# The state recurrence of a decoder layer: how the product with C is formed and summed

## The reference, cut to what matters

```python
proj = hidden_states @ W_in.T                      # 512 -> 2 x 1024
x, gate = (proj[..., :D_IN], proj[..., D_IN:])
...                                                # causal convolution of 4 taps
x = silu(xc)
ssm = x @ W_x.T                                    # 32 + 16 + 16 columns
ts, Bm, Cm = rms of each part
dt = softplus(ts @ W_dt.T + b_dt)
def step(state, inp):
    dt_t, B_t, C_t, u_t = inp
    dA = jnp.exp(dt_t[..., None] * A)
    state = state * dA + (dt_t * u_t)[..., None] * B_t[:, None, :]
    y = jnp.einsum('bdn,bn->bd', state, C_t)
    return (state, y)
y = ys + x * D
y = y * silu(gate)
return y @ W_out.T
```

## Time and profile before

| | |
|---|---|
| median of 3 runs | 1618.45 us (1616.8, 1620.61, 1618.45) |
| profiled execution, its own time | 1616.8 us, the lowest of the three runs |
| its span from first to last instruction | 1616.8 us, 14599 instructions |
| busy: PE, DVE, ACT, POOL | 1351.5, 1080.7, 595.1, 655.2 us |
| mean granted clock of PE | 0.936 |

### The profile page before, as it was taken

How to read it: one execution, slowest core, us unless ns; L and a number is a source line. 1 busy time by engine, 2 the same in 40 slices (tenths; PEclk the granted TensorE clock), 3 DMA queues, 4 the chain that set the end, 5 groups by cost and what they waited for, 6 DMA issues and landing times.

```text
span 1616.8 us, 14599 instructions
## 1 busy us (share of the span) xinstructions
PE 1351.5 (84%) x4824; PEld 805.4 (50%) x4824; DVE 1080.7 (67%) x1691; ACT 595.1 (37%) x1115; POOL 655.2 (41%) x469
## 2 busy tenths in 40 slices
PE   7956667678956757698889999979999999999996
PEld 5522222235512222244435555547887878877774
DVE  7399999938399999837865444346444446555566
ACT  4464343313454344202212322225444434444431
POOL 3276666513377676411117111135333333333321
PEclk9878998989869898999989999979999999999999
DMA  5320000012320000150011000013221112222110
GB/s 205 126 104 6 7 13 7 13 59 72 118 99 7 13 7 7 37 173 12 3 36 50 20 20 1 14 41 103 71 73 66 66 53 79 78 65 64 49 59 26
DMA packets 34169, 85.70 MB, mean 53 GB/s; under 512 B 3888, under 2 KB 4144, under 8 KB 31152
## 3 DMA queue, kind: packets, MB, share of 16 engines
q1 hardware_dynamic: 34096, 84.78, 15.7%
HBM read 82.54 MB, written 2.23 MB: 52 GB/s over the span
## 4 chain that ended last, share of the span: by engine, by line
PE 54%; DVE 15%; issue 5%; ACT 2%; POOL 1%; DMA 0%; POOLq 0%; DVEq 0%; ACTq 0%
PE psum L422 7%; PE psum L424 7%; PE psum L423 7%; DVE arena L1396 4%; PE psum L755 3%; DVE psum L1403 3%; PE psum L625 3%; PE psum L782 3%; PE psum L486 3%; PE psum L619 3%; PE psum L495 2%; PE psum L542 2%; PE psum L774 2%; DVE arena L1341 1%; PE psum L583 1%
## 5 line engine op out<-in xcount | busy, mean ns | idle before, releaser
L486 PE MATMUL psum<-arena,prm 128*128 128x512 f32 x512 | 289.2, 695 | 174.0 <-DVE arena L1396 173.4
L1145 POOL TENSOR_TENSOR arena<-arena 128x1024 f32<-128x1024 f32 x128 | 310.3, 2426 | 122.4 <-DVE psum L1403 121.1
L1403 DVE TENSOR_TENSOR_SCAN psum<-psum,arena 128x1024 f32<-128x1024 f32 x128 | 292.4, 2286 | 8.7 <-ACT psum L807 8.7
L1113 POOL TENSOR_TENSOR w_split<-arena,w_split 128x512 fp32r<-128x512 f32 x128 | 168.1, 1332 | 311.9 <-ACT w_split L807 311.8
L486 PEld LDWEIGHTS psum<-arena,prm 128*128 128x128 f32 x512 | 97.0, 210 | 366.1 <-DVE arena L1396 293.8
L807 ACT ACTIVATE arena<-psum 128x512 f32<-128x512 f32 (+2 forms) x180 | 101.4, 575 | 275.2 <-PE psum L511 62.5
L807 ACT ACTIVATE arena<-arena 128x512 f32<-128x512 f32 x112 | 69.2, 628 | 258.1 <-DVE arena L1609 224.0
L807 ACT ACTIVATE psum<-arena,amat 128x508 f32<-128x508 f32 x256 | 163.5, 670 | 0.0
L1396 DVE TENSOR_TENSOR arena<-psum,arena 128x1024 f32<-128x1024 f32 x128 | 154.7, 1209 | 0.5 <-PE psum L486 0.5
L807 ACT ACTIVATE arena<-psum,prm 128x512 f32<-128x512 f32 (+1 forms) x130 | 89.0, 696 | 127.4 <-PE psum L619 54.4
L1093 POOL TENSOR_TENSOR lnrs<-lnve,halfneg 128x1 f32<-128x1 f32 x48 | 29.9, 623 | 248.7 <-DVE lnve L1313 248.7
(11 more groups left out here) (218 smaller groups left out, 2382.5 us busy)
## 6 DMA issues: line engine op xcount, KB each, us to landing
arena<-bc_scratch SPq DMA_DIRECT2D x16, 1024.0 KB, 7.6
arena<-wq SPq DMA_DIRECT2D x64, 256.0 KB, 2.9
arena<-wo SPq DMA_DIRECT2D x64, 256.0 KB, 2.9
arena<-win SPq DMA_DIRECT2D x32, 256.0 KB, 2.7
arena<-wout SPq DMA_DIRECT2D x16, 256.0 KB, 2.6
arena<-xT SPq DMA_DIRECT2D x8, 256.0 KB, 5.4
x_tok<-xtok SPq DMA_DIRECT2D x1, 2048.0 KB, 7.8
arena<-ctxtok SPq DMA_DIRECT2D x1, 2048.0 KB, 8.8
```

The costliest lines, as they stand in the source:

```text
L486: last = mm(bank[6 + m % 2][:, :], ident, prod[:, i % 2, n, :], start=False, stop=(q == GS - 1 and n == NG - 1))
L1113: gp.tensor_tensor(out_, whole, hi.bitcast(F32), ALU.subtract).then_inc(done, 1)
L1145: gp.tensor_tensor(bu[:, i % 2, :, :], dtu[:, m % 2, :].unsqueeze(1).to_broadcast([P, NG, HT]), Brep[:, q * NG:(q + 1) * NG, :], ALU.mult) ...
L1403: v.tensor_tensor_scan(d, d, bu[:, i % 2, :, :].rearrange("p n t -> p (n t)"), 0.0, ALU.mult, ALU.add).then_inc(S.scan_done, 1)
```

## The change

The product with C no longer happens with channels on partitions. Each scanned state row is transposed by PE, so that time lies on partitions and C is one value per partition, and is scaled while it is copied out of PSUM. Then PE transposes it back and accumulates in PSUM in the same instruction.

A unit k is now one state row n of a pair of channel blocks (e = 0 and 1). There are 64 units in a pass, MP = 4 pairs of blocks by 16 rows.

- `Crep` and its four DMAs are gone; only B goes through DRAM.
- The scan (two of 512 columns per unit) reads `dA` in PSUM (three buffers of one bank) and writes `hst` in SBUF (four buffers). The zeros at the starts of the sequences are written once per pass instead of in each step, since the scan no longer overwrites them.
- `turn_state` on PE: eight transposes of 128 x 128 per unit, from `hst` to `hT`, three buffers of one bank, each with two of the four sequences. `weigh` scales them by `ssmn` into `hTs`: four operations of 128 x 256 per unit, on ACT, but in every fourth unit the second two are on DVE. `sum_state`: eight transposes back, accumulating in banks 6 and 7.
- The order on PE is turn (k, 0), sum (k-1), turn (k, 1), save where k % 16 is 1. The skip product comes after row 4 instead of first.
- `bu` has four buffers of 1024 columns and lies over the split weights, so POOL waits for the end of the input projection; `dtu` has four buffers; the gates of the two blocks of a pair come together.

The diff, cut to its core:

```diff
-dA = psum[:, 0:3 * NG * HT].rearrange("p (s n t) -> p s n t", s=3, n=NG)
+dA = psum[:, 0:3 * HT].rearrange("p (s t) -> p s t", s=3)
+hT = psum[:, 3 * HT:6 * HT].rearrange("p (s b e d) -> p s b e d", s=3, b=2, e=2)
 skip = sb("skip", [P, 2, P])
-zeros = sb("zeros", [P, NG * HB])
-bu = part(80, 2 * NG * HT).rearrange("p (s n t) -> p s n t", s=2, n=NG)
-prod = part(88, 2 * NG * HT).rearrange("p (s n t) -> p s n t", s=2, n=NG)
+zeros = sb("zeros", [P, 3 * HB])
+bu = part(40, 4 * NG * HT).rearrange("p (s n t) -> p s n t", s=4, n=NG)
+hst = part(88, 4 * HT).rearrange("p (s t) -> p s t", s=4)
+hTs = part(32, 2 * HB * 2 * P).rearrange("p (s b e d) -> p s b e d", s=2, b=HB, e=2)
...
+def by_dve(k, c):
+    return c == 1 and k % 4 == 3
+def weighed(k, c):
+    if by_dve(k, c):
+        return S.h_dve, k // 4 + 1
+    return S.h_act, 2 * k - k // 4 + c + 1
...
+        for q in range(4):
+            if q == 1:
+                sp.wait_ge(S.wi_lo, 16 * (h + 1))
+            load(Brep[:, q * 4:(q + 1) * 4, :].rearrange("p n t -> p (n t)"),
+                 scratch[h, q * 4:(q + 1) * 4, :].rearrange("n t -> (n t)").partition_broadcast(P),
+                 (S.b_in0, S.b_in1, S.b_in2, S.b_in3)[q])
...
+        def turn_state(k, e):
+            pe.wait_ge(S.scan_done, 2 * k + e + 1)
+            for c in range(2):
+                at = 2 * k + c
+                if at >= 3 and e == 0:
+                    pe.wait_ge(*weighed((at - 3) // 2, (at - 3) % 2))
+                for b in range(2 * c, 2 * c + 2):
+                    last = nc.tensor.transpose(hT[:, at % 3, b % 2, e, :],
+                                               hst[:, (2 * k + e) % 4, b * L:(b + 1) * L], ident)
+                if e or c:
+                    last.then_inc(S.h_turned, 1)
+        def sum_state(k):
+            n, i = k % NS, k // NS * 2
+            if n == 0 and i >= 2:
+                pe.wait_ge(S.y_done, i)
+            for b in range(HB):
+                if b % 2 == 0:
+                    pe.wait_ge(*weighed(k, b // 2))
+                for e in range(2):
+                    last = mm(bank[6 + e][:, b * L:(b + 1) * L], hTs[:, k % 2, b, e, :], ident,
+                              start=(n == 0 and b == 0), stop=(n == NS - 1 and b == HB - 1), is_transpose=True)
+            last.then_inc(S.ysum, 1)
+            if n == 4:
+                for e in range(2):
+                    pe.wait_ge(S.skip_done, i + e + 1)
+                    mm(bank[6 + e][:, :], skip[:, e, :], u[:, i % MD + e, :],
+                       start=False, stop=False).then_inc(S.skip_used, 1)
+        for k in range(h * MP * NS, (h + 1) * MP * NS):
+            turn_state(k, 0)
+            if k > h * MP * NS and k % NS != 1:
+                sum_state(k - 1)
+            turn_state(k, 1)
+            if k % NS == 1:
+                sum_state(k - 1)
+        sum_state((h + 1) * MP * NS - 1)
...
+        av(psum[:, 0:3 * HT].rearrange("p (s t) -> p s t", t=L)[:, :, 0:1], zeros[:, :].unsqueeze(2), ACT.Identity)
+        def decay(i):
+            k, e = i // 2, i % 2
+            m, n = (k // NS) % MP * 2 + e, k % NS
+            if n == 0:
+                act.wait_ge(S.dt_done, h * MD + m + 1)
+            if i >= 3:
+                act.wait_ge(S.scan_done, i - 2)
+            c = m * NS + n
+            av(dA[:, i % 3, :].rearrange("p (b t) -> p b t", b=HB)[:, :, 1:],
+               dt[:, m, :].rearrange("p (b t) -> p b t", b=HB)[:, :, 1:],
+               ACT.Exp, scale=amat[:, c:c + 1]).then_inc(S.dA_done, 1)
+        def skip_of(j, e):
+            i = h * MD + 2 * j + e
+            if i >= 2:
+                act.wait_ge(S.skip_used, i - 1)
+            av(skip[:, e, :], ident, ACT.Identity,
+               scale=pc("dskip")[:, 2 * j + e:2 * j + e + 1]).then_inc(S.skip_done, 1)
+        def weigh(k):
+            for c in range(2):
+                if by_dve(k, c):
+                    continue
+                act.wait_ge(S.h_turned, 3 * k + 2 + c)
+                if k >= 2 and c == 0:
+                    act.wait_ge(S.ysum, k - 1)
+                for b in range(2 * c, 2 * c + 2):
+                    last = av(hTs[:, k % 2, b, :, :], hT[:, (2 * k + c) % 3, b % 2, :, :], ACT.Identity,
+                              scale=ssmn[:, b, RK + NS + k % NS:RK + NS + k % NS + 1])
+                last.then_inc(S.h_act, 1)
+        first = h * MP * NS
+        for e in range(2):
+            skip_of(0, e)
+        for i in range(2 * first, 2 * first + 2):
+            decay(i)
+        for k in range(first, first + MP * NS):
+            for e in range(2):
+                if 2 * (k + 1) + e < 2 * (first + MP * NS):
+                    decay(2 * (k + 1) + e)
+            weigh(k)
+            if k - first < MD - EARLY:
+                exp_dt(k - first + EARLY)
+            if k - first == MD - EARLY:
+                for m in range(EARLY, MD):
+                    ln_dt(m)
+            if k % NS == 2 and k - first >= NS:
+                for e in range(2):
+                    skip_of((k - first) // NS, e)
...
+        pool.wait_ge(S.inproj, 16 * (h + 1))
+        for j in range(MP):
             for q in range(GS):
...
+                for e in range(2):
+                    i = (((h * MP + j) * GS) + q) * 2 + e
+                    if q == 0:
+                        pool.wait_ge(S.dtu_done, h * MD + 2 * j + e + 1)
+                    if j == 0 and EARLY <= 2 * q + e < MD:
+                        base(2 * q + e)
+                    if j == 0 and e == 0:
+                        pool.wait_ge((S.b_in0, S.b_in1, S.b_in2, S.b_in3)[q * NG // 4], 16 * (h + 1))
+                    if i >= 4:
+                        k = i // 2 - 2
+                        pool.wait_ge(S.scan_done, 2 * (k * NG + NG - 1) + e + 1)
+                    gp.tensor_tensor(bu[:, i % 4, :, :],
+                                     dtu[:, (h * MD + 2 * j + e) % 4, :].unsqueeze(1).to_broadcast([P, NG, HT]),
+                                     Brep[:, q * NG:(q + 1) * NG, :], ALU.mult).then_inc(S.bu_done, 1)
...
         def step_in(m):
...
+            i = h * MD + m
+            if i >= 4:
+                dve.wait_ge(S.bu_done, (i // 2 - 2) * 2 * GS + 2 * (GS - 1) + i % 2 + 1)
+            dve.wait_ge(S.dt_done, i + 1)
+            v.tensor_tensor(dtu[:, i % 4, :], dt[:, m, :], u[:, m, :], ALU.mult).then_inc(S.dtu_done, 1)
+        def weigh(k):
+            dve.wait_ge(S.h_turned, 3 * k + 3)
+            dve.wait_ge(S.ysum, k - 1)
+            for b in range(2, HB):
+                last = v.tensor_scalar(hTs[:, k % 2, b, :, :], hT[:, (2 * k + 1) % 3, b % 2, :, :],
+                                       ssmn[:, b, RK + NS + k % NS:RK + NS + k % NS + 1], None, ALU.mult)
+            last.then_inc(S.h_dve, 1)
         def scan(i):
+            k, e = i // 2, i % 2
             dve.wait_ge(S.dA_done, i + 1)
...
+            dve.wait_ge(S.bu_done, k // NG * 2 + e + 1)
+            if k >= 2:
+                dve.wait_ge(S.h_turned, 3 * (k - 2) + (3 if e else 1))
+            v.tensor_tensor_scan(hst[:, i % 4, :], dA[:, i % 3, :], bu[:, (k // NG * 2 + e) % 4, k % NG, :], 0.0,
                                  ALU.mult, ALU.add).then_inc(S.scan_done, 1)
         def finish_y(m):
...
+            dve.wait_ge(S.ysum, (h * MP + m // 2 + 1) * NS)
             v.tensor_tensor(g[:, m, :], bank[6 + m % 2][:, :], g[:, m, :], ALU.mult).then_inc(S.y_done, 1)
         for m in range(EARLY):
             one_plus(m)
...
+        for m in range(2):
+            step_size(m)
+            step_in(m)
+        first = h * MP * NS
+        for k in range(first, first + MP * NS):
+            j, n = (k - first) // NS, k % NS
+            scan(2 * k)
+            if k > first and by_dve(k - 1, 1):
+                weigh(k - 1)
+            if n == 1 and j >= 1:
+                finish_y(2 * j - 2)
+                finish_y(2 * j - 1)
+            scan(2 * k + 1)
+            if k - first < MD - EARLY:
+                one_plus(k - first + EARLY)
+            if n in (9, 11) and j + 1 < MP:
+                step_size(2 * (j + 1) + (n - 9) // 2)
+            if n in (10, 12) and j + 1 < MP:
+                step_in(2 * (j + 1) + (n - 10) // 2)
+        weigh(first + MP * NS - 1)
+        for m in range(MD - 2, MD):
+            finish_y(m)
```

More of the change, by code:

```diff
@@ L27 @@
 GS = NS // NG
+MP = MD // 2
 RK = 32
@@ L115, in decoder_kernel @@
                    loraA, loraBT, dwin, dw1, dw2, dwout, wq, wk, wv, wo, ra, bwT, out):
-    scratch = nc.dram_tensor("bc_scratch", [2, 2 * NS, HT], F32, kind="Internal").ap()
+    scratch = nc.dram_tensor("bc_scratch", [2, NS, HT], F32, kind="Internal").ap()
     with ExitStack() as ctx:
@@ L180, in decoder_kernel @@
         ssmsq = part(26, HB * SSM)
-        ssmn = part(27, HB * SSM).rearrange("p (b c) -> p b c", b=HB)
+        ssmn = part(60, HB * SSM).rearrange("p (b c) -> p b c", b=HB)
         ssmc = part(29, HT, SSM)
@@ L203, in decoder_kernel @@
         wdt_sb = part(162, DI, RK)
```

(61 more changed lines are left out.)

44 lines of the change are left out of this document (2 added, 42 removed).

## The result

The changed kernel takes 1636.28 us (median of four, 1635.61 to 1637.47) beside 1619.53 for the kernel before on the same chip: ratio 1.0106, 95% interval 1.0091 to 1.0121. The forecast was 1551. The profiled execution has a span of 1634.5 us.

What follows compares the result with a forecast made beforehand. DVE alone was taken to bound both recurrence passes. Each was to fall from 236.8 to 203 us, 33.9 less; twice is 67.8, with 0.8 for loads 67.0, giving 1551 us, range 1516 to 1607.

Steps and rivals of the forecast that it cites:

- First eight k: First eight units of a pass: DVE's pairs make six take 3.7 us instead of 2.8, +5.4; Ln block +4.9.
- how the engines interlock: Chain scan, turn, scale, turn back: an ordinary unit costs ACT's 2.74 us, every fourth 3.05; 180.3 us a pass.
- the Ln block: Six Ln and two table loads on ACT, 6.0 us, about 1.1 of it still hidden: +4.9 us a pass.
- the steps and gates on DVE are mostly covered: +1.9: DVE's step operations and gates in a pass: mostly covered by other work, adding 1.9 us.
- The prices: Times per operation: short scan 1.13 us, ACT scaling 0.38, DVE's two scalings 0.75, transpose 0.11 or 0.21 at low clock.
- rival 4: PE's sums take two instructions each, adding 90 us: 1640 us; chance 0.03.
- an ordinary group of four: Four units, one at 3.05 us and three at 2.74: 11.27 us, sixteen times in a pass.
- One sign named ahead: PE's clock would be over 0.9 after the first 15 us of a pass if the forecast was right.
- rival 2: DVE alone bounds the passes, with perfect overlap: 185 us a pass, 1516 us; chance 0.10.
- rival 3: PE's clock changes between its levels, low for half of each pass: 231.5 us a pass, 1607 us; chance 0.08.
- rival 1: PE stays at the low clock: 3.75 us a unit, 260 us a pass, 1664 us; chance 0.16.

Runs made afterwards that it cites:

- Exp edit: Changed kernel with six Exp a pass, which start dt of later blocks, put ahead of ACT's scalings instead of behind them: 1597 us.
- its edit alone: Changed kernel with POOL's differences for dt queued behind both products of a row pair, not each ahead of one: 1620.8 us.
- EARLY = 8: Changed kernel with EARLY 8 instead of 2, so dt's preparation for all eight blocks stands ahead of the recurrence: 1586.7 us.

## Why the prediction was wrong

The step that failed is "First eight k", in the words "DVE's pairs L1373 and L1375 (1.4 us each) make six of them 3.7 instead of 2.8, +5.4". It counts the pairs as DVE's own time and asks nothing of what they wait for. The part on how the engines interlock followed scan, turn, scaling and decay, and left out the Exp that stands behind the scalings in ACT's list and feeds these pairs. The diff had both, and asking what is queued on ACT behind the scaling, which waits for PE and through it for the newest scan, would have found it. Measured: 63.7 us for 32.9. Of the 30.8 us too many, 19.3 are the loop, as the Exp edit alone shows. The rest is divided up from the waits and not shown part by part: 7.2 are DVE's waits behind POOL's order (its edit alone took 6.1 off in this pass), 1.3 the skip product of row 4, and the other 3 smaller waits and the Ln block (one wait of 6.4 us in the run with the Exp ahead, for the 4.9 forecast). The pairs themselves, the term of the forecast, were cheaper than it had them: 1.07 us from L1441's start to the next scan's, not 1.4.

A second, smaller failure is "the steps and gates on DVE are mostly covered: +1.9" a pass. The three groups of rows 8 to 11 cost 8.5 us (14.1 against 11.27) and the block changes 5.1 (13.9, 12.5 and 12.5): 13.6. Of this the blocking between DVE and POOL explains 1.3 us in each of six `step_size`, 7.8. I had asked whether DVE slows POOL, and not the reverse. The block changes have a clock in them. In the run with EARLY = 8, PE's timeline there shows

```profile
156.68 0.69 PE L492 MATMUL psum<-prm,arena 128*128 128x128 f32 x4 [0.46 <-DVE arena L1473]
158.99 1.11 PE L492 MATMUL psum<-prm,arena 128*128 128x128 f32 x4 [1.61 <-DVE arena L1473]
159.90 1.91 PE L506 MATMUL psum<-prm,arena 128*128 128x128 f32 x8
...
169.36 1.04 PE L506 MATMUL psum<-prm,arena 128*128 128x128 f32 x8
```

Behind the pause of 1.6 us for the gates eight sums take 1.91 us instead of 1.04, and the granted clock is 0.50 from 160 to 165 us; in the 4.6 us from 152.0 it was 1.00. Within one pass this happens at one change and not at another (units of 5.7, 4.8 and 3.3 us), and why is open.

The prices held. A short scan lies 1.13 us from the next (forecast 1.13); four scalings on ACT take 1.57 us, about 0.37 each (0.38); DVE's pair 0.77 with the next scan's start (0.75); a transpose 0.11 and 0.21; a sum one instruction, eight in 1.04 (rival 4 falls); an ordinary group of four 11.2 to 11.5 us (11.27). ACT is busy for 173 us a pass (over 170) and POOL for 157 (159). One sign named ahead did not hold: the clock was to be over 0.9 after the first 15 us of a pass, and it was 0.58 over the first 64. The outcome was slower, for which I had given 0.18, but by none of the rivals: rival 2 needed DVE without idle time, rival 3 a clock that is low for half of a pass, and rival 1, at 1664, PE at the low clock throughout.

Rival 1 is refuted by the table above: 0.96 over 181 us in which PE makes transposes and, three times, the skip products; and in a stretch with transposes alone:

```profile
180.00:184.00 4.00, 2.93 (x25) 2.46 (x24) 3.66 (x6) 3.03 (x6) 3.84 (x2) 1.00 0.00 0
```

The rule of the Trainium skill ("TensorE: Matmul & The Clock Gate", Part 4: PE-mode transpose), that the full clock does not engage for transposes, disagrees with this trace, and the measurement decides. The clock was low where PE was half busy (31 of 63.7 us), and there it followed from the loop more than it made it: with EARLY = 8 the same eight units have 0.82 without any edit on PE.

## What to carry to other kernels

When a change puts an operation that waits for the newest result into an engine's list, look at everything behind it in that list, however small, and ask who waits for it: six Exp of 0.6 us cost 19 us a pass, and moving them ahead of the waiting operation turned a loss of 1% into a gain of 1.3%. A wait that is taken away by running two engines side by side can come back as a slower operation: see in the row of each whether its duration stays. Read a pass in quarters or sixteenths, not by its mean; here an eighth of the units held over two thirds of the miss.

## What the runs showed of the hardware that was not expected

- A VectorE operation of 128x512 with its operands in SBUF takes 0.43 us (L1442) or 0.69 us (L1444) beside an idle GpSimd, and up to 1.34 and 2.72 us when GpSimd's 128x1024 product is running; L1444 and L1449 end 0.6 us after that product. GpSimd's two products in a row in turn take 5.13 us instead of 4.69 where such an operation falls between them. An operation that is moved out of the way can push the next one into it (`step_in`, 0.66 us, then 1.84).
- Transposes of f32 hold the full clock, 0.11 us apart (clock 1.00 from 180 to 184 us of the changed kernel). In the kernel with EARLY = 8 a pause of 1.6 us in an otherwise busy stretch was followed by some 7 us of transposes 0.21 us apart.
